# A convolution and feed-forward block on one core: the second part of a pair's input load moved behind the round trip of the means

## The reference, cut to what matters

```python
x = x + _L0_conv_ref(_ln_c(x), ...)     # channel norm, then sign(), 3x3 conv with sign weights,
                                        # batch norm over all 32 images, relu
t = _to_tokens(x)
t = t + _L0_ffn_ref(_ln_t(t), ...)      # router, top half of the tokens, 128 -> 512 -> 128 with gelu
...
def _L0_conv_ref(x, w, b, gamma, beta):
    xa = sign_a(x)
    wq = quant_weight_W2(w)
    y = jax.lax.conv_general_dilated(xa, wq, window_strides=(1, 1), padding=[(1, 1), (1, 1)], ...)
    mean = jnp.mean(y, axis=(0, 2, 3), keepdims=True)
    var = jnp.var(y, axis=(0, 2, 3), keepdims=True)
```

## Time and profile before

| | us |
|---|---|
| median of 3 runs | 2020.09 (2017.94 to 2023.11) |
| profiled execution | 2015.51 |
| its span, first to last instruction | 2013.7 |
| PE busy in the span | 1852.1 (92%) |
| DVE, ACT, POOL busy | 1568.3, 1214.9, 1143.0 |

### The profile page before, as it was taken

The page is one execution under the profiler, slowest core; times in us unless marked ns, Lnnn a source line. Parts: engine busy times, 40 slices in busy tenths (PEclk is TensorE's granted clock), DMA queues, the critical chain, the costliest instruction groups (busy, mean ns, idle before and its releaser), DMA issues.

```text
span 2013.7 us, 32702 instructions
## 1 busy us (share of the span) xinstructions
PE 1852.1 (92%) x8507; PEld 992.6 (49%) x8507; DVE 1568.3 (78%) x4488; ACT 1214.9 (60%) x2030; POOL 1143.0 (57%) x907
## 2 busy tenths in 40 slices
PE   7789989759999999999999999999999999999996
PEld 4557666634444444444444444444444444444443
DVE  3487677867888788888888888888888888888875
ACT  5466666446666566666666666666666666666653
POOL 3465666364655556556565556665666555555543
PEclk8899999969999999999999999999999999999998
DMA  5677888511333333333333333333333333333213
GB/s 221 246 280 289 295 331 304 199 40 65 129 119 127 110 125 118 118 118 118 122 123 122 125 119 117 119 134 116 119 117 119 125 122 117 120 127 124 99 71 133
DMA packets 82074, 294.08 MB, mean 146 GB/s; under 512 B 23920, under 2 KB 28864, under 8 KB 81984
## 3 DMA queue, kind: packets, MB, share of 16 engines
q1 hardware_dynamic: 68880, 242.40, 33.0%
q10 hardware_dynamic: 13104, 50.72, 6.7%
HBM read 213.80 MB, written 78.07 MB: 145 GB/s over the span
## 4 chain that ended last, share of the span: by engine, by line
PE 51%; DMA 10%; DVE 6%; SPq 6%; issue 3%; POOL 1%; ACT 1%; ACTq 0%; DVEq 0%; POOLq 0%
PE ps L1168 25%; PE ps L1157 6%; PE ps L1158 5%; PE ps L1159 5%; PE ps L1113 5%; SPq L504 4%; DMA wse<-w_row 4%; DMA w_row<-wrow 3%; PE ps L1146 2%; DMA y16a<-y_int 2%; DMA y16b<-y_int 2%; SPq L510 1%; DVE base L910 1%; POOL rm L592 1%; ACT hs L670 1%
## 5 line engine op out<-in xcount | busy, mean ns | idle before, releaser
L1168 PE MATMUL ps<-hs,w_c 128*128 128x448 f32 x1792 | 765.9, 555 | 0.4 <-ACT yo L680 0.4
L670 ACT ACTIVATE hs<-ps,b1c,undo 128x448 f32<-128x448 f32 x896 | 609.8, 719 | 128.6 <-PE ps L1159 121.7
L578 POOL TENSOR_TENSOR tl<-tr,th 128x448 f16<-128x448 f32 x224 | 243.7, 1089 | 306.1 <-PE ps L1159 187.7
L1168 PEld LDWEIGHTS ps<-hs,w_c 128*128 128x128 f32 x1792 | 313.9, 191 | 209.3 <-issue 177.6
L573 POOL TENSOR_TENSOR xb<-xb,zr 128x448 f32<-128x448 f32 x224 | 261.4, 1169 | 265.6 <-ACT zr L697 264.9
L1157 PE MATMUL ps<-th,w_h 128*128 128x448 f16 x896 | 318.4, 355 | 17.0 <-ACT hs L670 17.0
L585 POOL TENSOR_TENSOR yo<-yo,base 128x448 f32<-128x448 f32 x221 | 277.1, 1260 | 75.6 <-DVE yo L987 75.6
L1159 PE MATMUL ps<-th,w_l 128*128 128x448 f16 x896 | 316.1, 353 | 0.0
L1158 PE MATMUL ps<-tl,w_h 128*128 128x448 f16 x896 | 316.1, 353 | 0.0
L680 ACT ACTIVATE yo<-ps,cols 128x448 f32<-128x448 f32 x224 | 141.7, 633 | 240.0 <-PE ps L1168 239.8
L1074 PE MATMUL ps<-packs,cwT 128*128 128x448 f32 x1008 | 245.9, 397 | 1.7 <-DVE y16a L759 1.7
(11 more groups left out here) (146 smaller groups left out, 2376.5 us busy)
## 6 DMA issues: line engine op xcount, KB each, us to landing
xb<-x SPq DMA_DIRECT2D x48, 896.0 KB, 4.6
xb<-x SPq DMA_DIRECT2D x48, 672.0 KB, 4.4
result<-yo SPq DMA_DIRECT2D x32, 896.0 KB, 3.5
gate_all<-gate_row ACTq DMA_DIRECT2D x31, 896.0 KB, 4.4
result<-yo SPq DMA_DIRECT2D x32, 672.0 KB, 3.0
gate_all<-gate_row ACTq DMA_DIRECT2D x31, 672.0 KB, 5.5
base<-x SPq DMA_DIRECT2D x16, 896.0 KB, 10.1
hs<-mean_row SPq DMA_DIRECT2D x14, 896.0 KB, 5.1
```

The source lines that it names most:

```text
L578: nc.gpsimd.tensor_tensor(cut(tl, c), tr[(b + c) % 2][:, :], cut(th, c), ALU.subtract).then_inc(tl_ready, 1)
L670: nc.scalar.activation(hs[(b + slot) % 2][:, j, :], ps[:, H_BANK + j, 0:T], ACT.Gelu_apprx_tanh, bias=b1c[:, j:j + 1], scale=undo[:, 1:2]) ...
L1168: last = M(bank, w2_c[:, j, :], hs[(b + c) % 2][:, j, :], start=first, stop=final)
```

## The change

Three statements of SP's `phase1(p)` change their order. Before, the second part of pair p + 2 (in the last periods: the whole x of the second phase's first two images) was issued first, then the store of the second part of y of pair p - 1, then the round trip of the means of pair p + 2. Now the store comes first, the round trip next, and the second part of x follows them, in front of the store of the first part of y of pair p. No transfer, instruction or wait is added or taken away, and the other engines' programs are the same.

```diff
             def phase1(p):
+                if p:
+                    store_y(p - 1, 1)
+                if MEAN_FROM <= p + 2 < NP:
+                    for n in (2 * p + 4, 2 * p + 5):
+                        save_mean(n)
                 if p + 2 <= NP:
                     sp.wait_ge(signed, (p + 1) * 2 * NCH)
                     if p + 2 < NP:
...
                         for b in range(2):
                             for part in range(2):
                                 load_x(b, b, part)
-                if p:
-                    store_y(p - 1, 1)
-                if MEAN_FROM <= p + 2 < NP:
-                    for n in (2 * p + 4, 2 * p + 5):
-                        save_mean(n)
                 store_y(p, 0)
                 if p + 3 < NP:
                     sp.wait_ge(signed, (p + 1) * 2 * NCH + 2 * HALF)
```

## The result

| | us |
|---|---|
| after, median of 4 runs | 2045.34 (2037.5 to 2049.02) |
| before, median of 4 runs | 2019.01 (2015.58 to 2023.11) |
| ratio after to before | 1.0124, 95% interval 1.0089 to 1.016 |
| profiled execution after, and its span | 2046.05, 2044.3 |

What follows compares the result with a forecast made beforehand. A circle of transfers and waits in the first phase was taken to bound the kernel. +21.6 (twelve periods) + 3.2 (step before) - 1 (phase end) = +23.8 us, rounded to 2043 us; range 2016 to 2054 us.

Steps and rivals of the forecast that it cites:

- Something goes round in a circle: First phase: neither PE nor DMA engines are full; means' load, next x, PE's means, write and round trip wait in turn.
- 3.2 us for the second part of x: SP's queue: moved before the next pair's first part, it delays that landing by 3.2 us a period, bounds 0 and 6.5.
- no difference: Rival: the means' last load regains its speed, 2.1 us back each period; -3.5 us in all, 2016 to 2024 us; chance 0.18.
- The round trip: Means written and loaded back: 5.7 us in every period, the gain from shortening bounded by 0 and 1.1 us a period.
- The first leg: Start of the means' round trip: 1.65 us throughout, instead of 2.72 us when the DMA engines are still at work.
- Making the means: From PE's start on the means to SP's write: 1.95 us, with nothing added by the change.
- the forecast 287.4 us: Twelve first-phase periods at 23.95 us each, against 265.8 us before: +21.6 us.
- a period that is already long for other reasons takes in some of the 3.2 us: Reason given for rounding the forecast time from 2043.9 down to 2043 us.
- No late second part: PE's line 1051: the second part of x still lands before it is read, so its lateness costs nothing.
- the end of the phase: The store of y's second part goes before the second phase's x loads; ACT's 0.60 us idle goes: -1 us, 0 to -2.
- 50 us or more: Sign of being right: PE's waits at line 1062 for x grow from 21 us to this.
- The upper end of the forecast, +32 us: Top of the forecast range +14 to +32 us, chance 0.68, from a second part of x between 2.5 and 4 us.

Runs made afterwards that it cites:

- E2: Against the changed kernel, the second part of x changes places with the store of y's first part, going behind it: 2046.12 us, ratio 1.0147.
- E4: Against the changed kernel, only the second image's second part of x stays behind the means; the first image's goes in front: 2028.81 us, ratio 1.0059.
- E1: Against the changed kernel, the second part of x goes back in front of the means, behind the store of y's second part: 2016.31 us, ratio 0.9984.
- E3: Against the changed kernel, the second part of x goes behind the next pair's first part: 2014.58 us, ratio 0.9984.
- E5: Order of the kernel before, but both images' means are written, waited for once and loaded together: 2005.87 us, ratio 0.9927.
- E7: Against the kernel before, second part of x behind the next pair's first part, and both images' means making their round trip together: 1999.44 us, ratio 0.9893.
- E8: Against the kernel before, the next pair's first part goes in front of the store of y's first part: 2044.49 us, ratio 1.0123.

## Why the prediction was right

**The bound.** "Something goes round in a circle" held: what is put into it costs (E2, E4), what is put beside it is free (E1, E3), and taking something out of it gains (E5 to E7). It is not paid or gained in full. The length from the last load to the means grew by 3.0 us in E2 and 1.9 in E4, the period by 2.2 and 1.1; from the first write to PE's means 1.3 us went in E5 and 1.6 in E7, the period fell by 0.8 and 0.9. The other links give part of it back, as the terms below show for the change.

**3.2 us for the second part of x.** The length grew from 13.1 to 16.3 us, as forecast. By what path it got there differs in part. These are stretches after: 241 to 244 us holds the last load of the means, the next one the second part of x, then the store, then the next pair's first part.

```profile
241.00:244.00 3.00, 3.00 (x14) 2.25 (x13) 1.40 (x3) 1.89 (x4) 1.30 (x2) 1.00 0.90 327
244.00:249.70 5.70, 5.70 (x24) 4.22 (x23) 3.54 (x6) 3.65 (x7) 1.23 (x2) 1.00 0.94 303
...
252.00:256.20 4.20, 2.01 (x10) 1.47 (x8) 3.41 (x6) 4.03 (x9) 4.20 (x5) 1.00 1.00 405
```

The first premise of the rival "no difference" came true, its result did not. The last load of the means moves at 327 GB/s instead of 213. It lands 4.4 us after its issue, where the one issued at 222.24 before took 6.1 (first the kernel after, then the one before):

```profile
DMA to landing us min/median/max: 4.4/4.4/4.4
...
DMA to landing us min/median/max: 6.1/6.1/6.1
```

But the second part of x behind it, now the load next to the store, falls to 303 GB/s, and its window shows

```profile
L404 SPq DMA_DIRECT2D base<-x x2: 432/432/432, 240.6 to 241.1; - x2
...
DMA to landing us min/median/max: 6.6/7.7/8.7
```

so it lands at 249.8 us, 5.2 us behind the means (244.6) and not 3.2. It takes 2.0 us more than was taken, and the load in front of it 1.7 us less. The prediction kept the slow load slow and x at full speed; that the two differences nearly cancel and leave the 3.2 us taken from x's own rows was luck. In E2, where the store stands between the two, both hold: the load of the means is slow again and the growth is 3.0 us. By the Trainium skill's limit of about 358 GB/s ("DMA: Bandwidth & Descriptors", Specifications) the second part would have taken 3.84 us, an estimate. The traces do not agree with that limit: in E2 it moves at 413 GB/s, in the last stretch of that run shown below.

**The round trip.** The first leg is 1.7 us on average, as forecast; the whole is 5.84 us instead of 5.7. Before it was 6.23.

**Making the means.** 1.95 us were taken, from one period. Over the twelve periods the mean before is 2.9 us, since DVE often had chunks to decode in front of the copy: at PE's start of 99.50 us before, for instance, the copy came 3.8 us later.

```profile
103.32 1.15 DVE L745 COPY ur<-ps 128x448 f32<-128x448 f32 x2
```

After, making the means takes 1.7 to 2.5 us, in one period 6.2 us, and 2.4 us in the mean.

**The period.** Its three terms in the mean of the twelve periods:

| us | before | forecast | after |
|---|---|---|---|
| last load of the means to PE's means | 13.1 | 16.3 | 16.3 |
| making the means, to the first write | 2.9 | 1.95 | 2.4 |
| round trip, first write to last load | 6.2 | 5.7 | 5.8 |
| period | 22.15 | 23.95 | 24.55 |

The forecast set the measured period of 22.15 us against a sum in which making the means stood at 1.95 us, and so took 0.9 us a period off for it without a reason; half of that came. This is the term that was mis-sized: 0.46 us in each of twelve periods, 5.5 of the 7.2 us by which they exceed the forecast 287.4 us. Most of it stands in one period. The last ten of the twelve have 24.05 us, (377.22 - 136.74) / 10, from SP's timeline:

```profile
107.85 0.50 SPq L432 DMA_DIRECT2D mean_row<-ur  x1
...
136.74 0.50 SPq L432 DMA_DIRECT2D mean_row<-ur  x1
...
377.22 0.50 SPq L432 DMA_DIRECT2D mean_row<-ur  x1
```

The period from 107.85 to 136.74 is the one with 6.2 us. For it the prediction rounded its sum down, "a period that is already long for other reasons takes in some of the 3.2 us"; it took in nothing, and has 28.9 us after and 25.5 us before. DVE prepares tables there; its timeline after:

```profile
130.01 1.04 DVE L818 TENSOR_TENSOR cand<-neg_b,candc 128x1 f32<-128x1 f32 x1
...
136.10 1.15 DVE L745 COPY ur<-ps 128x448 f32<-128x448 f32 x2
```

The tables end at 131.05 us, half a microsecond after PE has started its means (130.54), and three chunks and the copy follow. The same stood there before, 7 us earlier (end of line 818 at 123.76, copy at 128.79): the tables begin when DVE is done with the chunks in front of them, and those ended 7 us later too. They moved back with the circle and so were no cover. The period before that one has 25.2 us, since its second leg lasted 4.9 us, where most take about 4. If these two were as long as the other ten, the twelve periods would come to 288.6 us, near the forecast 287.4; they came to 294.6.

**No late second part, and the end of the phase.** Both held: no wait for x at line 1051. From the last means to the second phase's end the time is 0.6 us shorter than before, where 1 us had been taken. The idle of the earlier trace rows is gone: the last half of that store now lands 5.3 us after its issue at 391.2, and the same start of ACT has no idle in front of it.

```profile
403.88 0.52 ACT L647 ACTIVATE y16b<-ps 128x448 int16<-128x448 f32 x1
```

**PE's waits.** "50 us or more" at line 1062 was too much: they are 40.6 us. The twelve periods grew by 28.8 us; in them PE waits 19.3 us longer for x and is busy 10.3 us longer (254.0 against 243.7 us), at a granted clock of 0.92 instead of 0.97. The sum had no term for the clock. In five of the twelve pairs after, PE's means begin at 1.2 GHz behind a wait for x, as in the first of them (clock: third number from the end of the stretch):

```profile
105.41 3.21 PE L1062 MATMUL ps<-xb,kt 128*32 128x448 f32 x16 [4.03 <-DMA xb<-x]
...
107.20 0.62 DVE L745 COPY ur<-ps 128x448 f32<-128x448 f32 x1 [1.13 <-PE ps L1062]
...
105.50:107.00 1.50, 1.50 (x12) 0.40 (x16) 0.57 (x1) 0.98 (x2) 1.50 (x2) 0.50 0.55 217
```

There DVE's copy waits for PE, and SP's write comes 2.44 us after PE's start; in four pairs whose means begin at full clock it comes after 1.68 us. So the low clock is inside the circle there, with 0.76 us. The rest of PE's longer busy time did not set the period, since PE still waits for x at the end of each one.

The sum for the whole was 23.8 us; medians differ by 26.3 us, the spans of the two profiled executions by 30.6 us, and the interval of the ratio means 18 to 32 us. So the median lies nearer to the forecast than the profiled periods do, which is luck too. The upper end of the forecast, +32 us, is 2 us below what its own 4 us for the second part give (23.8 + 13 x 0.8 = 34.2); the result does not hang on it.

## What to carry to other kernels

Where transfers of one queue run one behind another, the place of a transfer is paid by whoever stands behind it. Before moving one, follow the circle once round (write, wait, load, the loads behind it, the engine that starts on them) and see whether the new place lies in it; that the moved transfer itself has time to spare says nothing. And an engine's idle gap is worth filling only if what fills it is no longer in front of something that is waited for: here the gap was the wait for the round trip, and making the two round trips at once was worth more than any order of the loads tried here.

## What the runs showed of the hardware that was not expected

A load shortly in front of the store of y's first part ran slow, whichever load it was. In the kernel before and in E2, where the store is issued directly behind the last load of the means, that load lands 6.1 and 5.8 us after its issue, and moves at 213 and 219 GB/s. E2's stretch with that load, and the one with the second part of x behind the store:

```profile
239.50:243.50 4.00, 4.00 (x17) 2.71 (x15) 2.34 (x5) 2.63 (x5) 1.59 (x2) 1.00 0.98 219
245.80:249.00 3.20, 3.20 (x14) 2.44 (x13) 1.77 (x3) 1.94 (x4) 0.82 (x2) 1.00 1.03 413
```

With the store further back (the change, E8) the load of the means lands after 4.4 and 4.5 us, and the load next to the store is the slow one, in E8 the end of the next pair's first part at 292 GB/s:

```profile
235.50:238.00 2.50, 2.50 (x11) 1.78 (x10) 2.36 (x5) 1.38 (x4) 1.04 (x1) 1.00 0.88 370
...
240.00:243.00 3.00, 3.00 (x16) 2.69 (x15) 0.00 (x0) 0.00 (x0) 3.00 (x4) 1.00 0.97 292
```

The DMA engines count as busy all the while (shares of 0.94 to 0.98 in the slow stretches). The store of y's second part behind x had no such effect in the stretches read: after the change x moves at 405 GB/s in front of it (252.00 to 256.20). Why is open; no run here took the store away.
